# A fused linear-attention and mixture-of-experts layer on eight cores: the start-up reordered, with matmuls on a zero tile ahead of it

## The reference, cut to what matters

```
xn = layernorm(x)                                  # over the 1024 features
q = elu(xn @ W_Q.T) + 1;  k = elu(xn @ W_K.T) + 1;  v = xn @ W_V.T      # 8 heads of 64
S_t = g*S_(t-1) + k_t v_t^T;  z_t = g*z_(t-1) + k_t;  g = sigmoid(decay_log)
y_t = (S_t^T q_t) / (z_t.q_t + 1e-6) * sigmoid(xn @ W_g.T + b_g)
attn = y @ W_O.T
ffn = xn @ W_lin.T + b_lin + sum over the top 2 of 8 experts: weight_e * (xn @ left_e) @ right_e
out = x + attn + ffn
```

## Time and profile before

| what | us |
|---|---|
| median of 3 runs | 261.59 (261.1 to 263.84) |
| the profiled execution, device time | 263.04 |
| its span on the slowest core (core 5) | 262.0 |
| spans of the eight cores | 258.1 to 262.0 |
| TensorE busy on core 5 | 238.8 (91%) |
| VectorE, ScalarE, GpSimd busy | 162.4, 76.0, 61.7 |

### The profile page before, as it was taken

How to read it: one execution, slowest core, us unless ns; L and a number is a source line. 1 busy time by engine, 2 the same in 40 slices (tenths; PEclk the granted TensorE clock), 3 DMA queues, 4 the chain that set the end, 5 groups by cost and what they waited for, 6 DMA issues and landing times.

```text
span 262.0 us, 5276 instructions; the slowest of 8 cores (258.1 to 262.0 us)
## 1 busy us (share of the span) xinstructions
PE 238.8 (91%) x1688; PEld 117.4 (45%) x1688; DVE 162.4 (62%) x425; ACT 76.0 (29%) x128; POOL 61.7 (24%) x99
## 2 busy tenths in 40 slices
PE   0348999999897999999999999999999999999995
PEld 0223454454453555444454555444545454445442
DVE  5365457658857657666566657557566776687522
ACT  2563765576163323312322021111111201000000
POOL 2761100011134230505050402112214030333000
PEclk9999999999999999999999999999999999999999
DMA  6999999999986226352327232233222224343423
GB/s 174 207 175 255 251 169 206 233 181 180 245 219 102 83 60 184 101 155 67 118 78 129 83 101 83 88 94 103 81 100 83 101 83 124 136 140 108 159 104 136
DMA packets 20366, 35.86 MB, mean 137 GB/s; under 512 B 12210, under 2 KB 12530, under 8 KB 20084
## 3 DMA queue, kind: packets, MB, share of 16 engines
q1 hardware_dynamic: 17444, 24.89, 32.9%
q0 software_dynamic: 2896, 10.64, 21.5%
...
## 4 chain that ended last, share of the span: by engine, by line
PE 84%; DVE 6%; DMA 4%; issue 3%; ACT 1%; SPq 0%; DVEq 0%; ACTq 0%
PE PJ L365 26%; PE L L387 17%; PE L L431 9%; PE PJ L358 7%; PE PJ L387 4%; PE L L365 4%; DMA x_sb<-x 4%; PE PJ L431 2%; PE L L358 2%; PE T L336 2%; PE SY L379 2%; PE SY L403 2%; PE T L344 1%; PE T L417 1%; PE SY L407 1%
## 5 line engine op out<-in xcount | busy, mean ns | idle before, releaser
L387 PE MATMUL L<-wlin_sb,xnfm 128*128 128x512 bf16 x208 | 49.2, 379 | 0.0
L323 POOL TENSOR_SCALAR S_blk<-S_sb,small_s 128x260 bf16<-128x260 f32 x30 | 28.6, 969 | 82.7 <-DVE S_sb L814 82.5
L387 PEld LDWEIGHTS L<-wlin_sb,xnfm 128*128 128x128 bf16 x208 | 20.0, 98 | 24.1 <-issue 0.8
L885 ACT ACTIVATE e_sb<-PJ 128x512 bf16<-128x512 f32 x28 | 16.5, 594 | 41.2 <-PE PJ L365 39.7
L643 DVE TENSOR_SCALAR e_sb<-e_sb 128x512 bf16<-128x512 bf16 x32 | 9.7, 303 | 30.0 <-ACT e_sb L885 30.0
L861 ACT ACTIVATE xn_tm<-x_sb,nmr,rstd 128x1024 bf16<-128x1024 f32 x16 | 19.9, 1245 | 25.4 <-POOL nmr L279 23.8
L431 PE MATMUL L<-wo_sb,ygfm 128*128 128x512 bf16 x104 | 26.7, 379 | 0.0
L365 PE MATMUL PJ<-xnfm,wq_sb 128*128 128x512 bf16 x112 | 26.6, 380 | 0.0
L365 PE MATMUL PJ<-xnfm,wg_sb 128*128 128x512 bf16 x112 | 26.6, 379 | 0.0
L365 PE MATMUL PJ<-xnfm,wk_sb 128*128 128x512 bf16 x112 | 26.6, 380 | 0.0
L358 PE MATMUL PJ<-wv_sb,xnfm 128*128 128x512 bf16 x96 | 24.6, 400 | 0.0
...
## 6 DMA issues: line engine op xcount, KB each, us to landing
ro_sb<-x SPq DMA_DIRECT2D x16, 512.0 KB, 4.0
out<-ro_sb SPq DMA_DIRECT2D x15, 512.0 KB, 2.7
x_sb<-x SPq DMA_DIRECT2D x10, 512.0 KB, 9.1
x_sb<-x POOLq DMA_DIRECT2D x6, 512.0 KB, 20.5
...
wv_sb<-wv POOLq DMA_DIRECT2D x4, 256.0 KB, 11.8
wq_sb<-wq POOLq DMA_DIRECT2D x2, 512.0 KB, 17.6
wk_sb<-wk POOLq DMA_DIRECT2D x2, 512.0 KB, 24.4
```

What stands on the lines that cost most here:

```text
L323: GP.tensor_scalar(S_blk[:, :].rearrange("p (q w) -> p q w", q=4)[:, :, 65 * e : 65 * e + 65], S_sb[:, :].rearrange("p (q w) -> p q w", q= ...
L387: TE.matmul(lb(c, n)[:, :], xnk(k, c), wlin_sb[:, D * k + 512 * n : D * k + 512 * n + 512], start=False, stop=False)
L885: SE.activation(e_sb[:, 512 * (n % 2) : 512 * (n % 2) + 512], bank[:, :], AF.Exp).then_inc(ac_e, 1)
```

## The change

Start-up and slots 0 and 1 alone are rewritten; from slot 2 on TensorE's list is as it was.

- TensorE runs 22 matmuls of 128x512 on the zeroed `S_blk` at the beginning, 6 between the transpositions of x0 and x1, and 3 and 4 between the first v projections (`warm`). Their results are not read.
- The identity, the small and the mask constants are one array `cst` (467 floats a row, 239 KB), issued by ScalarE, followed by x2, also by ScalarE. SyncE issues x0, x1, x3. VectorE copies identity and small constants out of `cst` behind stats(0), and waits there for `cst`.
- GpSimd starts its loads when VectorE's memsets are done and no longer waits for x0. wq, wk and wg come in quarters, x4 to x7 one after each half of a weight. GpSimd computes scale and bias of chunks 1 and 3, and its later loads stand behind them.
- v goes by chunk (0, 1, 2, then 3), v4 to v7 stand between the parts of q, k and the gate; the banks come from a ring of six, and ktr of chunks 0 and 1 writes to L1 and L0.
- In slots 0 and 1 the gate projection stands ahead of `ytr` (before: at the end of the slot), and ktr(1) no longer waits for the gate product. `top2b(0)` and stats(9) move into slot 0 on VectorE; rs(9), rs(10), rs(11) stand behind the `S_blk` and `SG_sb` products on GpSimd; xn(9) moves into slot 0 on ScalarE.

The diff, cut; in the programs of TensorE and ScalarE most removed lines are left out:

```diff
-    ident_d = din("ident", [128, 128], BF16)
-    small_d = din("small", [128, 19])
-    cmat_d = din("cmat", [128, 384])
+    cst_d = din("cst", [128, 467])
...
+    cst = th_g[:, 0:467]
...
-    ring4 = [PJ[0], PJ[1], L[0], L[1]]
+    KT = [L[1][:, 0:256].bitcast(BF16), L[0][:, 0:256].bitcast(BF16),
+          T1[:, 0:512], T1[:, 0:512]]
+    ring6 = [PJ[0], PJ[1], L[0], L[1], SYb[0], SYb[1]]
+    vb = [ring6[i] for i in (0, 1, 2, 3, 2, 0, 5, 2)]
+    qb = [ring6[i] for i in (4, 5, 0, 1)]
+    kb = [ring6[i] for i in (3, 4, 5, 2)]
+    gb = [ring6[i] for i in (3, 4, 0, 1)]
...
         load_x(1)
-        SY.dma_start(ident[:, :], ident_d[:, :]).then_inc(d_id, 16)
-        load_x(2)
         load_x(3)
-        SY.dma_start(small[:, :], small_d[:, :]).then_inc(d_sm, 16)
-        SY.dma_start(cmat, cmat_d[:, :]).then_inc(d_cm, 16)
         SY.dma_start(bl32[32:33, 0:512], blin_d[:, 0:512]).then_inc(d_bl, 16)
         SY.dma_start(bl32[96:97, 0:512], blin_d[:, 512:1024]).then_inc(d_bl, 16)
-        SY.wait_ge(d_wg[1], 16)
+        SY.wait_ge(d_wg[3], 16)
         load_x(10)
         load_x(11)
...
         GP.memset(mhalf[:, :], -0.5).then_inc(po_ini, 1)
-        GP.wait_ge(d_x[0], 16)
+        GP.wait_ge(po_ini, 1)
+        GP.wait_ge(dv_ini, 3)
         for i in range(4):
-            o = 2 * FH * i
-            GP.dma_start(wv_sb[:, o : o + 2 * FH], wv_d[:, o : o + 2 * FH]).then_inc(d_wv[i], 16)
-        wload_half(wq_sb, wq_d, 0, d_wq)
+            wload_q(wv_sb, wv_d, i, d_wv)
+        rs(1)
+        wload_q(wq_sb, wq_d, 0, d_wq)
+        wload_q(wq_sb, wq_d, 1, d_wq)
         xload(4)
+        rs(3)
+        wload_q(wq_sb, wq_d, 2, d_wq)
+        wload_q(wq_sb, wq_d, 3, d_wq)
         xload(5)
-        wload_half(wq_sb, wq_d, 1, d_wq)
+        wload_q(wk_sb, wk_d, 0, d_wk)
+        wload_q(wk_sb, wk_d, 1, d_wk)
         xload(6)
+        wload_q(wk_sb, wk_d, 2, d_wk)
+        wload_q(wk_sb, wk_d, 3, d_wk)
         xload(7)
-        wload_half(wk_sb, wk_d, 0, d_wk)
-        wload_half(wk_sb, wk_d, 1, d_wk)
+        wload_q(wg_sb, wg_d, 0, d_wg)
+        wload_q(wg_sb, wg_d, 1, d_wg)
         wload(lg_sb, lg_d, d_lg)
-        wload_half(wg_sb, wg_d, 0, d_wg)
-        wload_half(wg_sb, wg_d, 1, d_wg)
+        wload_q(wg_sb, wg_d, 2, d_wg)
+        wload_q(wg_sb, wg_d, 3, d_wg)
...
-        rs(9)
         for c in range(NCH):
-            if c + 10 < NCH:
+            if c + 10 < NCH and c >= LAG:
...
+            if c == 0:
+                rs(9)
+            if c < LAG:
+                rs(c + 10)
...
+    def warm(n):
+        for _ in range(n):
+            TE.matmul(SYb[1][:, :], S_blk[:, 0:128], S_blk[:, 0:512], start=True, stop=True)
...
-            ins = TE.transpose(T1[:, 128 * p : 128 * p + 128], fmc(kfm, c)[:, p, :],
+            ins = TE.transpose(KT[c][:, 128 * p : 128 * p + 128], fmc(kfm, c)[:, p, :],
...
+    def gproj(c):
+        TE.wait_ge(dv_k, c + 5)
+        fproj(wg_sb, c // 4 + 1, c % 4, PJ[1], pe_g)
...
+        TE.wait_ge(dv_z, 1)
+        warm(22)
+        TE.wait_ge(dv_id, 1)
         xtr(0)
+        warm(6)
         xtr(1)
         TE.wait_ge(dv_xev, 1)
+        TE.wait_ge(d_wv[0], 16)
+        vproj(0, vb[0], 0, 2)
+        warm(3)
+        TE.wait_ge(d_wv[1], 16)
+        vproj(0, vb[0], 2, 4)
+        warm(4)
+        TE.wait_ge(dv_xev, 2)
+        vproj(1, vb[1], 0, 4)
         xtr(2)
+        TE.wait_ge(d_wv[2], 16)
+        for c in range(2):
+            vproj(c, vb[c], 4, 6)
         TE.wait_ge(dv_xev, 3)
+        vproj(2, vb[2], 0, 6)
+        xtr(3)
+        TE.wait_ge(d_wv[3], 16)
+        for c in range(3):
+            vproj(c, vb[c], 6, 8)
         TE.wait_ge(dv_xev, 4)
+        vproj(3, vb[3])
+        for i in range(4):
+            TE.wait_ge(d_wq[i], 16)
+            if i == 3:
+                xtr(4)
+            for m in range(4):
+                if i == 0 and m >= 2:
+                    TE.wait_ge(ac_v, m - 1)
+                fproj(wq_sb, 0, m, qb[m], pe_q, 2 * i, 2 * i + 2)
+        TE.wait_ge(dv_xev, 5)
+        TE.wait_ge(ac_v, 3)
+        vproj(4, vb[4])
+        for i in range(4):
+            TE.wait_ge(d_wk[i], 16)
+            if i == 3:
+                xtr(5)
+            for m in range(4):
+                if i == 0 and m == 0:
+                    TE.wait_ge(ac_v, 4)
+                elif i == 0 and m < 3:
+                    TE.wait_ge(dv_q, m)
+                elif i == 0:
+                    TE.wait_ge(ac_v, 5)
+                fproj(wk_sb, 0, m, kb[m], pe_k, 2 * i, 2 * i + 2)
         TE.wait_ge(dv_xev, 6)
+        TE.wait_ge(dv_q, 3)
+        vproj(5, vb[5])
+        for i in range(4):
+            TE.wait_ge(d_wg[i], 16)
+            if i == 3:
+                TE.wait_ge(dv_xev, 7)
+                TE.wait_ge(dv_k, 3)
+                vproj(6, vb[6])
+                xtr(7)
+            for m in range(4):
+                if i == 0 and m < 2:
+                    TE.wait_ge(dv_k, m + 1)
+                elif i == 0 and m == 2:
+                    TE.wait_ge(ac_v, 6)
+                elif i == 0:
+                    TE.wait_ge(dv_q, 4)
+                fproj(wg_sb, 0, m, gb[m], pe_g, 2 * i, 2 * i + 2)
+            if i == 1:
+                xtr(6)
         TE.wait_ge(d_lg, 16)
         tgp(0)
+        TE.wait_ge(dv_xev, 8)
+        TE.wait_ge(dv_k, 4)
+        vproj(7, vb[7])
...
             if c == 0:
-                TE.wait_ge(dv_xev, 8)
+                TE.wait_ge(ac_g, 1)
+            elif c < LAG:
+                TE.wait_ge(ac_v, 8)
             elif c < 4:
                 TE.wait_ge(dv_gate, c)
             if c < 4:
                 ktr(c)
             if c > 0:
                 TE.wait_ge(dv_norm, c)
+            else:
+                TE.wait_ge(ac_g, 2)
+                TE.wait_ge(ac_v, 7)
             scores(c)
             if lo >= 0:
                 right_pair(lo)
...
             av(c)
             if c < NCH - 1:
                 TE.wait_ge(dv_ktm, c + 1)
-                if c >= 4:
+                if c == 0:
+                    TE.wait_ge(dv_xev, 8)
+                elif c < LAG or c >= 4:
                     TE.wait_ge(dv_gate, c)
                 state(c)
             if lo >= 0:
...
                     kproj(c)
                 o_group(lo, 0)
                 lin_group(lo, 1)
-            elif c + 8 < NCH:
+            else:
                 vslot(c)
+                gproj(c)
             TE.wait_ge(dv_norm, c + 1)
...
-            if more:
-                TE.wait_ge(dv_k, c + 5)
-                fproj(wg_sb, b + 1, s, PJ[1], pe_g)
+            if lo >= 0 and more:
+                gproj(c)
     def dve_program():
+        VE.memset(S_blk[:, :], 0.0).then_inc(dv_z, 1)
-        VE.memset(S_blk[:, :], 0.0)
         VE.wait_ge(dv_ini, 2)
...
                   1.0).then_inc(dv_ini, 1)
         stats(0)
+        VE.wait_ge(d_cm, 16)
+        VE.tensor_copy(ident[:, :], cst[:, 403:467].bitcast(BF16)).then_inc(dv_id, 1)
+        VE.tensor_copy(small[:, :], cst[:, 384:403]).then_inc(dv_sm, 1)
         stats(1)
         stats(2)
         xev_v(0)
         stats(3)
         xev_v(1)
+        VE.wait_ge(dv_sm, 1)
+        VE.tensor_scalar(gb_h[:, :], small[:, 0:4], 0.5, None, ALU.mult).then_inc(dv_ini, 1)
         xev_v(2)
-        xev_v(3)
-        VE.wait_ge(d_sm, 16)
-        VE.tensor_scalar(gb_h[:, :], small[:, 0:4], 0.5, None, ALU.mult).then_inc(dv_ini, 1)
...
-        VE.wait_ge(d_cm, 16)
+        xev_v(3)
...
         ins.then_inc(dv_mk, 1)
         stats(4)
-        stats(5)
         xev_v(4)
-        for m in range(2):
-            phi(m, ring4[m], fm(qfm, 0)[:, 512 * m : 512 * m + 512], dv_q)
+        for m in range(4):
+            if m == 2:
+                stats(5)
+            phi(m, qb[m], fm(qfm, 0)[:, 512 * m : 512 * m + 512], dv_q)
+        stats(6)
         xev_v(5)
-        for m in range(2, 4):
-            phi(m, ring4[m], fm(qfm, 0)[:, 512 * m : 512 * m + 512], dv_q)
-        stats(6)
+        for m in range(4):
+            phi(4 + m, kb[m], fm(kfm, 0)[:, 512 * m : 512 * m + 512], dv_k)
         stats(7)
-        VE.wait_ge(ac_mk, 1)
+        xev_v(6)
+        VE.wait_ge(ac_dec, 3)
         qt(0)
-        for m in range(4):
-            phi(4 + m, ring4[(m + 2) % 4], fm(kfm, 0)[:, 512 * m : 512 * m + 512], dv_k)
-        xev_v(6)
         xev_v(7)
         stats(8)
         top2a(0)
-        stats(9)
-        top2b(0)
         VE.wait_ge(po_dk, 1)
         for c in range(NCH):
             b, s = c // 4, c % 4
...
             more = c < NCH - 4
             if c < 4:
                 VE.wait_ge(pe_ktr, c + 1)
-                ktile = T1[:, 0:512]
+                ktile = KT[c]
...
             VE.wait_ge(pe_sc, c + 1)
+            if c == 0:
+                VE.wait_ge(ac_mk, 1)
             VE.tensor_tensor(A_sb[:, 0:512], SYb[0][:, :], masks[:, 0:512], ALU.mult)
             VE.tensor_tensor(A_sb[:, 512:1024], SYb[1][:, :], masks[:, 512:1024],
                              ALU.mult).then_inc(dv_mask, 1)
```

(46 more changed lines are left out.)

93 lines of the change are left out of this document (18 added, 75 removed).

## The result

The changed kernel takes 268.56 us (median of 4 runs, 266.94 to 269.73), the kernel before 261.35 beside it on the same chip: ratio 1.0246, 95% interval 1.0209 to 1.0284. It is 2.5% slower; the forecast was 258.2, and 255.2 to 261.6 as the range. The profiled execution of after is its fastest, 266.94 us, and what follows is read from it; in the other three the slowest core had a span of 266.8 to 268.6 us, and what held it up was not traced.

What follows compares the result with a forecast made beforehand. TensorE's path up to slot 2 on slowest core 5 was taken to bound the kernel; 5.4 + 0.6 - 2.0 = 4.0 us gained gave 259.0, or 257.6 off the median, and 258.2 was taken, range 255.2 to 261.6.

Steps and rivals of the forecast that it cites:

- the first term: Start-up to the q projection: q starts at 24.2 instead of 29.6, 5.4 us gained, 3.8 by clock and 1.6 by order.
- The last term: Slots 0 and 1: they take 24.6 instead of 22.6 us, a loss of 2.0.
- the second: From q to slot 0: 30.3 us against the measured 30.9, bringing slot 0's gain to 6.0; the sum's 0.6.
- I take the measured 12.2 as it was, as the same bytes must pass.: Start-up loads: x2 arrives at 12.2 as before; bounds a microsecond earlier or 1.5 later.
- Constants at 7.5: Start-up: constants land at 7.5; VectorE's wait for them ahead of x1's statistics costs nothing up to 10.5.
- Clock term: Start-up, v phase: zero matmuls raise TensorE's clock before v and it stays up, 3.8 us gained.
- the clock falls back: Start-up: TensorE idles between about 11 and 14.8 and its clock drops; about 3 us lost, 261.2, chance 0.18.
- Order term: Start-up up to q: the new order of work gains 1.6 us of the 5.4.
- Second stretch: From the q projection to slot 0: the same matmuls take 30.3 us, measured 30.9 before.
- The cushion of the weights: Ahead of slot 0: last gate weights land at 45.5, are waited for at 48.0, so 2.5 us to spare.
- Third stretch: Slots 0 and 1: 16.1 us to the tanh plus 8.5 to slot 2, 24.6 instead of 22.6; bounds 22 and 26.
- it hides under it: Slot 1 to slot 2: the moved gate projection does not shorten VectorE's 8.5 us path, which covers it.

Runs made afterwards that it cites:

- e6: The changed start-up with slots 0 and 1 as before, and x2 issued by SyncE between x1 and x3; ratio 1.0039 to the kernel before.
- e14: e13 with x1's statistics on VectorE put ahead of the wait for the constants; ratio 1.0022 to the kernel before.
- e13: e6 with v's projection of x6 put back behind the router, and ScalarE's copy of it behind the gate's tanh; ratio 1.0047 to the kernel before.
- e4: The kernel before with zero matmuls alone: 22 ahead of x0's transposition, 6 ahead of x1's and 7 behind it; ratio 0.9966.
- e15: e14 with x10 and x11 requested when wk's last quarter has landed instead of wg's; ratio 1.0015 to the kernel before.
- e3: The kernel before with only the gate projection moved ahead of ytr in slots 0 and 1; ratio 1.0058.
- e9: e3 with eight matmuls that nobody reads added behind slot 1's ytr, where TensorE was idle; ratio 1.0007 to the kernel before.
- e8: e4 with x10 and x11 requested when wk has landed instead of wg; ratio 0.9964 to the kernel before.

## Why the prediction was wrong

Its sum was 5.4 + 0.6 - 2.0. The failed step is the first term: q was to start at 24.2 and started at 27.0 to 29.4. The last term had the right sign and mechanism and was too small. On the slowest core (7) slot 2 starts at 87.05 instead of 79.1. Of these 8.0 us, 5.2 are the first term, 0.5 the second and 2.3 the third. Of the 5.2, 2.8 arise because v starts at 17.60 instead of 14.8 (x2 is late), 2.0 because its first matmuls and the zero matmuls between them run at the low level (17.60 to 21.98, 4.4 us for a forecast of 2.4), and 0.4 behind that.

- *"I take the measured 12.2 as it was, as the same bytes must pass."* x2's statistics began at 13.2 to 14.8. The same bytes pass, but not in the same order: x2 now stands behind 239 KB of constants and beside wv's packets. The upper bound that I gave, 1.5 later, was exceeded by a microsecond on core 7. `e6` puts the price of x2's place at 1.1%.
- *Constants at 7.5, "costs nothing until they land at 10.5".* They landed at 9.6 on core 7, within that bound, and cost all the same: x1's statistics, GpSimd's rs(1) and the wq loads behind it (issued at 13.16, before at 7.55) hang on it. Without the wait (`e14` against `e13`) the wq loads are issued at 9.9 to 12.1 instead of 11.7 to 14.9, v starts 1.8 and q 1.1 us earlier, in traces; the 0.25% in the ratio the intervals don't separate.
- *Clock term, 3.8 us.* The mechanism is real (`e4`), and what it gives depends on what stands behind the zero matmuls. In the changed order TensorE idles 2.10 and 2.04 us ahead of v on core 7, and v begins at the low level there and on five more cores, and falls to it soon on the other two: the rival "the clock falls back", as described, on top of a late x2. With x2 early (`e6`) v stays at the high level on four cores. `e4` had q 1.4 us earlier in the mean, and 0.3% in time, which is not clear of nothing.
- *Order term, 1.6 us.* None, and not only because x2 was late. Where v runs at the high level throughout, the new order takes 9.8 to 10.0 us from v to q (`e6`, four cores; 9.4 forecast), the old one 8.5 to 9.2 (`e4`, seven cores). `e6` starts v 1.2 us earlier than `e4` in the mean and q 0.4 us later. Seven zero matmuls, 1.5 us at 0.215 each, stand inside v in the new order; no run takes out those alone.
- *Second stretch, 30.3.* 30.8 on core 7. Right within half a microsecond. The cushion of the weights was not tested there, as the start was late. With an early start TensorE waits up to 0.8 us for weights (`e14`), and up to 2.44 when x10 is asked for earlier as well (`e15`).
- *Third stretch, 24.6.* 26.9 to 27.5. Term by term from s = 60.18: state s + 8.7 (8.1 forecast), rs(9) s + 12.9 (12.2), xn(9) s + 14.3 (13.7), tanh s + 16.8 (16.1): right in order, 0.7 late. Then two things not in it: x9's transposition behind thr puts the k projection at s + 17.3, and the clock falls in the idle of 4.15 us, so that k and what follows take 9.6 instead of 8.5. Moreover 1.7 us of the slots' length, in the runs with slots as before, came from v's projection of x6 ahead of the router, a move that I had costed at nothing in the second stretch. The changed kernel's router part stands inside slot 0, so whether this order costs anything there was not tested.
- *The moved gate projection, "it hides under it".* Right, for the slot and, in the changed kernel, for what follows: slot 2 to the end takes as long as before. That was luck, as the sum had no term for it: in the kernel before the same move joins two idles into one, the clock falls behind it on seven cores, and it costs 0.6% (`e3`, `e9`).
- *x10's floor* is real: `e4` and `e14` run into it. The changed kernel does not, as its slots start late: VectorE waits for x10 on no core. So the spans came closer together (2.1 us instead of 3.9) as forecast, but not for the reason given. *Anything else unchanged* held: 178.9 before and 178.8 after, in the mean.
- The slower side had 0.06, all on late constants. Its mechanism, a wait of VectorE ahead of x1's statistics and x0's copy, was a part of the case. It was given too small a chance because several delays of the start-up lie in one chain, and I had costed each against x2 at 12.2.

What remains open: `e8`, the fastest version run, is 0.4% faster than before, at the edge of what can be told; why its median lies 1 us above its profiled execution (260.03) was not traced: in those runs the slowest core shows a granted clock of 0.986 to 0.993.
